# Head roots as a TensorE product, a reordered batch step and epilogues moved into the feed-forward tiles

## The chip, the cores and the metric

The kernel runs on one NeuronCore of a Trainium2 chip. The metric is the device time of one execution in microseconds (us), the median of three runs. Engines: PE (TensorE), DVE (VectorE), ACT (ScalarE), POOL (GpSimd) and SP (the queue that issues most DMAs).

## What is computed

The input is 8 sequences of 256 rows of 512. First comes an mLSTM cross attention with 16 heads of 32, whose query is the normalised `x` and whose keys and values are both `ctx`; then a feed-forward network (FFN) whose activations and weights are quantised in blocks of 32.

```python
Cn = C / (normalizer + EPS)
h = jnp.einsum('bhst,bhtd->bhsd', Cn, vh)
mu = h.mean(-1, keepdims=True)
var = ((h - mu) ** 2).mean(-1, keepdims=True)
hn = (h - mu) * jax.lax.rsqrt(var + EPS)
hn = hn * ln_scale.reshape(1, nh, 1, dh)
...
x = x + _L0_xattn_ref(_layernorm(x, axis=-1), ctx_2048, ctx_2048, ...)
x = x + _L0_ffn_ref(_layernorm(x, axis=-1), ...)
```

## The kernel before, in words

The work is tiled by 128 rows, so a sequence b has two chunks. Every engine has its instructions written out by hand in program order, and each runs them first in, first out; semaphores tie them together. There is no scheduler. An instruction that waits holds back all that stands behind it on its engine.

There are four stretches.

1. **Loading** (`pre_step`, eight times): x is normalised (`x_stats` on DVE, `x_rsqrt` on POOL, `x_norm` on ACT), x and ctx are transposed on PE, the gate products (`gates`) are accumulated, and one unit of the FFN's down weights is quantised per step. A weight unit passes through `w_front`, `w_pow`, `w_round` (DVE), `round_const` (ACT), `w_back` (POOL), `w_transpose` (PE) and an evacuation (ACT).
2. **Gates**: short operations on ACT and DVE turn the gates into decay tables; these go to DRAM and come back as `movt` and `statt` (`load_decay`).
3. **Batch steps** (`step`, b = 0 to 7). On PE: `heads` for chunk 0 (four, n = 0 to 3), `decay` 4 and 5, `centre`, `qk`, `x_transpose`, `state`, `decay` 6 and 7, `heads` for chunk 1 (n = 4 to 7), `inter`, a weight transpose, and then `decay` and `qk` of the next sequence. ACT takes exponentials of the decays (`exps`) and copies PSUM out (`copy_h`, `copy_v`, `copy_state`). DVE multiplies scores and decays (`c_mult`, four and four). Beside this the epilogue of the sequence before runs: `square` (ACT), `head_var` (DVE), `head_power` (ACT), `head_rsqrt` (POOL), `head_norm` (DVE, L1040), the product with the layer scale (POOL, L616), the residual (POOL, L621), `x1_stats` (DVE), `x1_rsqrt` (POOL), `x1_norm` (ACT, L826), `x1_round` (DVE), `back_x` (POOL). Two weight units are quantised in each step.
4. **FFN**: 16 tiles, each in two halves h. Per half PE does `p_transpose` of the tile before, `gate`, `up` and `down` of the tile before; ACT does `silu` and copies; DVE does `pair` (L1104, the block maxima, L1113, L1116); POOL does `back_p` (L679). The epilogue of sequence 7 and the rounding of sequence 6 run around the first tiles.

`settle` adds one to a semaphore nobody waits on. `ch.link` makes an engine wait for its own last instruction.

## Time and profile before

| | us |
|---|---|
| median of three runs | 553.61 |
| lowest, highest | 552.74, 558.61 |
| the profiled execution | 553.07 |
| its span, first to last instruction | 551.3 |

```profile
PE 454.0 (82%) x3465; PEld 300.7 (55%) x3465; DVE 432.6 (78%) x615; ACT 244.9 (44%) x343; POOL 245.2 (44%) x231
PE   0597795599789696969788785399999999999984
DVE  3769888478797897978787965997788788788880
POOL 2444531323635536273736563543454443443433
PEclk9767886589859586776859697899999999999996
```

The first line gives each engine's busy time and share of the span. The others cut the span into 40 slices; a digit is the busy share in tenths (PEclk: the granted TensorE clock, in tenths of 2.4 GHz). The batch steps are slices 8 to 24, where the clock digit swings once per step; the FFN is slices 25 to 40.

### The profile page before, as it was taken

What the parts mean: (1) busy time and instruction counts of PE and PEld (TensorE: products, weight loads), DVE (VectorE), ACT (ScalarE), POOL (GpSimd) and SP (SyncE); (2) the same over time, 40 slices, a digit from 0 to 9 for tenths busy, and PEclk for the clock granted to TensorE, in tenths of its full rate; (3) what the DMA queues carried; (4) which work ended last, traced back from release to release, by engine and by line L of the source; (5) the groups of instructions that cost most, each with busy time, mean ns of one, the idle gap of its engine ahead of it and who ended that gap; (6) DMA issues with size and microseconds to landing.
All of it is one profiled execution on the core that took longest, in us unless ns stands there. A gap on an engine that the chain in (4) does not pass through costs nothing.

```text
span 551.3 us, 10415 instructions
## 1 busy us (share of the span) xinstructions
PE 454.0 (82%) x3465; PEld 300.7 (55%) x3465; DVE 432.6 (78%) x615; ACT 244.9 (44%) x343; POOL 245.2 (44%) x231
## 2 busy tenths in 40 slices
PE   0597795599789696969788785399999999999984
PEld 0497795287657484757566562144444444444441
DVE  3769888478797897978787965997788788788880
ACT  2466664247264353545364544234434344344341
POOL 2444531323635536273736563543454443443433
PEclk9767886589859586776859697899999999999996
DMA  6655621412321414050421101201111111112111
GB/s 164 214 173 175 224 97 38 137 54 85 134 62 60 137 42 144 11 173 22 134 62 55 42 26 52 77 0 40 38 38 53 61 38 38 38 38 75 39 38 39
DMA packets 30564, 43.70 MB, mean 79 GB/s; under 512 B 6980, under 2 KB 11972, under 8 KB 30532
## 3 DMA queue, kind: packets, MB, share of 16 engines
q1 hardware_dynamic: 30532, 43.26, 24.3%
q8 instruction: 21, 0.34, 0.3%
q14 instruction: 11, 0.09, 0.1%
HBM read 34.41 MB, written 8.85 MB: 78 GB/s over the span
## 4 chain that ended last, share of the span: by engine, by line
PE 42%; issue 20%; POOL 17%; DVE 13%; ACT 4%; DMA 3%; POOLq 1%; SPq 1%; DVEq 0%; ACTq 0%
PE psA L1335 9%; PE psC L1362 9%; PE psA L1344 9%; PE psB L1354 3%; POOL wq L559 3%; POOL early L616 3%; PE psA L1234 2%; PE psC L1214 2%; DMA early<-in_x_dram 2%; POOL xc L649 2%; DVE wy L952 2%; DVE wq L955 1%; POOL qs L644 1%; PE psC L1173 1%; POOL rs L553 1%
## 5 line engine op out<-in xcount | busy, mean ns | idle before, releaser
L679 POOL TENSOR_TENSOR kTa<-kTa,ps 128x1024 bf16<-128x1024 bf16 x32 | 61.2, 1912 | 102.7 <-DVE kTa L1116 102.7
L1262 PE MATMUL psA<-vp,DC 128*128 128x128 f32 x512 | 73.7, 312 | 2.1 <-DVE DC L1019 2.1
L559 POOL TENSOR_TENSOR wq<-wq,ws 128x1024 bf16<-128x1024 bf16 x24 | 50.6, 2108 | 54.9 <-DVE wq L955 54.9
L1262 PEld LDWEIGHTS psA<-vp,DC 128*128 128x128 f32 x512 | 71.4, 227 | 4.0 <-issue 4.0
L1335 PE MATMUL psA<-WgT,qTa 128*128 128x512 bf16 x256 | 63.7, 394 | 7.5 <-ACT hf L813 3.9
L1362 PE MATMUL psC<-WdT,kTa 128*128 128x512 bf16 x256 | 62.2, 387 | 2.4 <-ACT kTa L879 2.4
L1344 PE MATMUL psA<-WuT,qTa 128*128 128x512 bf16 x256 | 61.3, 383 | 0.0
L879 ACT ACTIVATE kTa<-psB 128x1024 bf16<-128x1024 bf16 x32 | 32.8, 1024 | 54.5 <-PE psB L1354 54.2
L1019 DVE SCALAR_TENSOR_TENSOR DC<-psA,DC 128x512 f32<-128x512 f32 x64 | 41.7, 686 | 15.7 <-PE psA L1234 8.3
L1104 DVE TENSOR_TENSOR kTa<-kTa,psA 128x1024 f32<-128x1024 f32 x32 | 39.0, 1220 | 18.2 <-PE psA L1344 18.2
L804 ACT ACTIVATE DC<-psB 128x512 f32<-128x512 f32 x64 | 37.6, 597 | 23.6 <-PE psB L1248 23.2
L1113 DVE TENSOR_TENSOR qTa<-kTa,pinv 128x1024 fp8e4<-128x1024 f32 x32 | 41.1, 1285 | 4.9 <-DVE pinv L933 4.3
L1362 PEld LDWEIGHTS psC<-WdT,kTa 128*128 128x128 bf16 x256 | 25.3, 99 | 33.4 <-issue 3.1
L873 ACT ACTIVATE kTa<-psA 128x1024 f32<-128x1024 f32 x32 | 32.8, 1024 | 23.7 <-PE psA L1335 23.7
L1344 PEld LDWEIGHTS psA<-WuT,qTa 128*128 (+1 forms) x256 | 25.3, 99 | 31.3 <-issue 2.0
L1335 PEld LDWEIGHTS psA<-WgT,qTa 128*128 (+1 forms) x256 | 24.4, 101 | 32.3 <-ACT hf L813 4.0
L1182 PE MATMUL psC<-identb,wq 128*128 128x128 bf16 x192 | 21.3, 279 | 24.3 <-POOL wq L559 24.3
L927 DVE TENSOR_REDUCE pam<-kTa 128x32 f32<-128x1024 f32 x32 | 39.0, 1220 | 1.1
L1234 PE MATMUL psA<-qTa,kTa 32*128 32x128 f32 x512 | 25.4, 349 | 12.8 <-ACT hf L813 12.8
L1246 PE MATMUL psB<-mask,identb 128*128 128x512 bf16 x64 | 30.5, 477 | 5.7 <-DMA statt<-gate_split_scratch 5.7
L726 ACT ACTIVATE wm<-wm,wbase 128x1024 f32<-128x1024 f32 x24 | 27.5, 1147 | 16.1 <-DVE wm L947 16.1
L826 ACT ACTIVATE early<-early,nb,rs 128x512 f32<-128x512 f32 x16 | 12.1, 806 | 50.6 <-POOL nb L554 50.6
(131 smaller groups left out, 849.7 us busy)
## 6 DMA issues: line engine op xcount, KB each, us to landing
early<-in_x_dram SPq DMA_DIRECT2D x16, 512.0 KB, 4.1
early<-in_ctx_dram SPq DMA_DIRECT2D x8, 512.0 KB, 4.6
wraw<-in_L_ffn_w_down_dram SPq DMA_DIRECT2D x8, 512.0 KB, 5.5
wraw<-in_L_ffn_w_gate_dram SPq DMA_DIRECT2D x8, 512.0 KB, 4.2
...
```

Source lines behind the costliest of these rows:

```text
L559: nc.gpsimd.tensor_tensor(blocks(wq[p][:, :]), blocks(wq[p][:, :]), spread(ws4[p][:, :], UB), ALU.mult).then_inc(wq_ready.sem, 1)
L679: nc.gpsimd.tensor_tensor(blocks(pd[h]), blocks(pc[h]), spread(ps4[h][:, :], PB), ALU.mult).then_inc(pq_ready.sem, 1)
L804: nc.scalar.activation(DC[n % DCN][:, :], psB[n % 2][:, :], ACT.Exp).then_inc(d_exp.sem, 1)
L927: return nc.vector.tensor_reduce(am, src, AX.X, ALU.max, apply_absolute_value=True)
L1019: nc.vector.scalar_tensor_tensor(out=DC[n % DCN][:, :], in0=psA[:, n % HPC, :], scalar=float(DH) ** -0.5, in1=DC[n % DCN][:, :], op0=ALU.m ...
L1104: nc.vector.tensor_tensor(pr, sg, psA[:, PC:2 * PC, :].rearrange("p a b -> p (a b)"), ALU.mult).then_inc(p_ready.sem, 1)
L1113: fch.link(nc.vector.tensor_tensor(blocks(p8), blocks(pr), spread(pinv[:, :], PB), ALU.mult, saturate=False))
L1234: last = nc.tensor.matmul(psA[:, j, i4 * P:(i4 + 1) * P], kTa[r, b, i4, c * P:(c + 1) * P], qTa[r, b, i4, c * P:(c + 1) * P], start=True, ...
L1262: last = nc.tensor.matmul(psA[:, j, to:to + P], DC[n % DCN][:, i4 * P:(i4 + 1) * P], values[:, left:left + P], start=i4 == 0, stop=c == 0, ...
L1335: last = nc.tensor.matmul(psA[:, a, :], xqT[q][:, b, c * P:(c + 1) * P], WgT[:, c, h * PW + a * E:h * PW + (a + 1) * E], start=c == 0, sto ...
L1344: last = nc.tensor.matmul(psA[:, PC + a, :], xqT[q][:, b, c * P:(c + 1) * P], WuT[:, c, h * PW + a * E:h * PW + (a + 1) * E], start=c == 0 ...
L1362: last = nc.tensor.matmul(psC[p][:, :], pTs[h][:, k * P:(k + 1) * P], WdT[:, PK * h + k, :], start=h == 0 and k == 0, stop=h == 1 and k == ...
```

## The change

- **Roots times layer scale.** Before, DVE multiplied the heads by the roots (SBUF by SBUF, one operation of 128x1024) and POOL multiplied the result by the broadcast layer scale. Now PE transposes the roots of a sequence (`root_transpose`), ACT copies them out (`copy_root`), and PE multiplies them with a block-diagonal table `ltab` of the layer scale (`scale_root`, one fp32 product of 32x128 by 32x512 per chunk), which gives roots times scale as a matrix in PSUM. DVE multiplies each chunk of heads with it (`head_norm`, two of 128x512, PSUM by SBUF). POOL's product is gone.
- **The batch step** is put in another order on all engines. On PE the gate-weight transpose stands behind `decay` 5, the other weight transpose behind the next sequence's `qk` and `decay`s. On ACT `x1_norm` stands behind the next sequence's exponentials. On DVE `w_pow` stands between the two `head_norm`s and `w_front` ahead of `x1_stats`. On POOL `w_back` stands ahead of the residual.
- **Start.** The x, weight and ctx loads are issued in another order on SP and the small constants from ACT's queue; the layer-scale load is 32 rows instead of 128; POOL makes its tables after the second `x_rsqrt`; a decay waits only for its own chunk's loads; `qk(0, 0)` goes ahead of the first decay.
- **FFN.** `x1_round` of sequence 6 and the whole epilogue of sequence 7 are cut up and put between the `pair`s of tiles 0 to 6; `x_transpose` moves to tiles 5 and 9. The roots of sequence 7 come from a POOL power of 128x16 per chunk (`last_power`) instead of ACT's logarithm and exponential and POOL's refinement.

```diff
+            def last_power(b, c):
+                gp.wait_ge(hv_ready.sem, hv_ready.at(b, 1))
+                last = nc.gpsimd.tensor_tensor(sm[:, 0, c, :], sm[:, 3, c, :], mhalf[:, 0:1].broadcast_to([P, NH]), ALU.pow)
+                if c == NCH - 1:
+                    last.then_inc(hr_ready.sem, 1)
...
-                ch.link(nc.gpsimd.tensor_tensor(hn, hn, lns[:, :].unsqueeze(1).broadcast_to([P, NCH, E]), ALU.mult))
...
+            def copy_root(b):
+                act.wait_ge(r_mm.sem, r_mm.at(b, 0))
+                act.wait_ge(rt_mm.sem, rt_mm.at(b, 1))
+                nc.scalar.activation(rT[:, :], psC[1][0:DROW, 0:NCH * P], ACT.Copy).then_inc(rt_ev.sem, 1)
...
+            def head_norm(b, p, c, bank):
+
+                ve.wait_ge(r_mm.sem, r_mm.at(b, c + 1))
+                nc.vector.tensor_tensor(sq[:, c], hf[p][:, c, :, 0:DH],
+                                        psC[bank][:, :].rearrange("p (h d) -> p h d", d=DH),
                                         ALU.mult).then_inc(hn_ready.sem, 1)
...
+            def root_transpose(b):
+
+                root = sm[:, :, :, :].rearrange("p k c h -> p (k c h)")
+                pe.wait_ge(hr_ready.sem, hr_ready.at(b, 1))
+                for c in range(NCH):
+                    last = nc.tensor.transpose(psC[1][0:DROW, c * P:(c + 1) * P], root[:, c * NH:c * NH + DROW], ident[:, :])
+                last.then_inc(rt_mm.sem, 1)
+
+            def scale_root(b, c, bank):
+                pe.wait_ge(rt_ev.sem, rt_ev.at(b, 1))
+                nc.tensor.matmul(psC[bank][:, :], rT[:, c * P:(c + 1) * P], ltab[:, :], start=True, stop=True).then_inc(r_mm.sem, 1)
...
 def decay(b, p, n):
                 c, j = divmod(n, HPC)
-                if n == 0:
-                    pe.wait_ge(d_ld, 16 * NCH * (1 + SPLIT) * b + 16 * NCH * (1 + SPLIT))
+                if j == 0:
+                    pe.wait_ge(d_ld[p][c], 16 * (1 + SPLIT) * (b // 2 + 1))
```

POOL's batch step, and its FFN part up to the loop:

```diff
             def step(b, p, n, first, last):
                 if not first:
                     head_rsqrt(b - 1)
+                w_back(2 * b + B + 1, 1)
                 if not first:
                     residual(b - 1)
                 if not last:
                     carry_q(b + 1, 1 - p)
-                w_back(2 * b + B + 1, 1)
                 if not first:
                     x1_rsqrt(b - 1)
                 if not last:
+                    weigh(b + 1, 1 - p)
                     w_back(2 * b + B + 2, 0)
-                    weigh(b + 1, 1 - p)
...
+            back_p(0, 0)
+            last_power(B - 1, 0)
+            back_p(0, 1)
+            last_power(B - 1, 1)
+            back_p(1, 0)
+            back_p(1, 1)
             residual(B - 1)
```

DVE in the first FFN tiles:

```diff
             pair(0, 0)
+            head_var(B - 1, 1)
+            pair(0, 1)
+            pair(1, 0)
+            head_norm(B - 1, 1, 0, 1)
+            pair(1, 1)
+            head_norm(B - 1, 1, 1, 1)
+            pair(2, 0)
+            x1_amax(B - 2, fch)
+            pair(2, 1)
+            x1_scale(B - 2, fch)
+            pair(3, 0)
+            x1_clamp(B - 2)
+            pair(3, 1)
             x1_stats(B - 1)
```

**PE, the middle of a batch step.** `cen` is `centre`, `qTa,kTa` is `qk`, `xc` is `x_transpose`, `ctc` is `state`, `mask` and `movt` are the two products of a `decay`, `DC4` is the first of `heads` for chunk 1. Before:

```order
L1214 MATMUL psC0<-cen,kTa 128x128 x4
L1234 MATMUL psA<-qTa,kTa 128x128 x16
L1280 MATMUL psC1<-identb,xc 128x128 x8
L1224 MATMUL psC0<-vw,ctc 32x33 x16
L1246 MATMUL psB0<-mask,identb 128x512
L1248 MATMUL psB0<-movt,statt 128x512
L1246 MATMUL psB1<-mask,identb 128x512
L1248 MATMUL psB1<-movt,statt 128x512
L1262 MATMUL psA<-vp1,DC4 128x128 x4
```

The same place now, with `sm` for `root_transpose` and `ltab` for `scale_root`:

```order
L1292 MATMUL psC0<-cen,kTa 128x128 x4
L1312 MATMUL psA<-qTa,kTa 128x128 x16
L1366 MATMUL psC1<-ident,sm 32x128 x2
L1302 MATMUL psC0<-vw,ctc 32x33 x16
L1371 MATMUL psC1<-ltab,rT 128x512
L1324 MATMUL psB0<-mask,identb 128x512
L1326 MATMUL psB0<-movt,statt 128x512
L1324 MATMUL psB1<-mask,identb 128x512
L1326 MATMUL psB1<-movt,statt 128x512
L1371 MATMUL psC0<-ltab,rT 128x512
L1358 MATMUL psC1<-identb,xc 128x128 x8
L1340 MATMUL psA<-vp1,DC4 128x128 x4
```

Both root products now stand in front of the chunk 1 heads, the second behind two decays.

**DVE, the middle of a batch step.** `wq` ends `w_round`; `DC` is the first `c_mult` of chunk 1. Before:

```order
L952 SCALAR_TENSOR_TENSOR wy<-wy,wm 128x1024
L96 REGISTER_ALU
L954 REGISTER_ALU
L955 SCALAR_TENSOR_TENSOR wq<-wy,wm 128x1024
L1040 TENSOR_TENSOR early<-hf,sm 128x1024
L1017 REGISTER_ALU
L1019 SCALAR_TENSOR_TENSOR DC<-psA,DC 128x512
```

Now:

```order
L997 SCALAR_TENSOR_TENSOR wy<-wy,wm 128x1024
L96 REGISTER_ALU
L999 REGISTER_ALU
L1000 SCALAR_TENSOR_TENSOR wq<-wy,wm 128x1024
L1087 REGISTER_ALU
L1088 TENSOR_TENSOR early<-hf,psC 128x512
L990 REGISTER_ALU
L992 TENSOR_SCALAR wm<-wy 128x1024
L1088 TENSOR_TENSOR early<-hf,psC 128x512
L1064 REGISTER_ALU
L1066 SCALAR_TENSOR_TENSOR DC<-psA,DC 128x512
```

The chunk 1 `c_mult`s stand behind both `head_norm`s, and so behind both root products.

**ACT, the end of a batch step.** `early<-early,nb,rs` is `x1_norm`, `hf` is `copy_h` of chunk 1, `DC` an `exps` of the next sequence. Before:

```order
L726 ACTIVATE wm<-wm,wbase 128x1024
L826 ACTIVATE early<-early,nb,rs 128x512 x2
L813 ACTIVATE hf<-psA 128x4x4x33
L730 REGISTER_ALU
L731 REGISTER_ALU
L731 ACTIVATE WuT<-psC 128x4x256
L803 ISA
L804 ACTIVATE DC<-psB 128x512
```

Now:

```order
L832 REGISTER_ALU
L833 ACTIVATE DC<-psB 128x512
L832 REGISTER_ALU
L833 ACTIVATE DC<-psB 128x512
L860 ACTIVATE early<-early,nb,rs 128x512 x2
L759 REGISTER_ALU
L760 REGISTER_ALU
L760 ACTIVATE WuT<-psC 128x4x256
L854 ACTIVATE early<-hf 128x1024
```

`x1_norm` has moved from ahead of `copy_h` to behind the fourth exponential of the next sequence.

## Rows read from the trace of the kernel before

**Rows 1.** Windows: length, busy of PE, PEld, DVE, ACT, POOL, granted clock, DMA share, GB/s

```profile
129.75:159.55 29.80, 23.74 (x247) 18.29 (x245) 25.23 (x39) 14.21 (x24) 15.21 (x15) 0.83 0.31 99
159.55:313.27 153.72, 129.75 (x1241) 97.17 (x1240) 129.31 (x192) 74.01 (x116) 78.39 (x75) 0.72 0.25 80
313.27:335.36 22.09, 16.32 (x205) 12.88 (x205) 14.77 (x25) 12.31 (x21) 13.14 (x13) 0.96 0.15 48
335.36:442.10 106.74, 93.21 (x500) 43.73 (x501) 88.30 (x111) 40.43 (x45) 46.85 (x33) 0.94 0.12 40
```

**Rows 2.** Chain of waits inside one batch step: start us, us, what

```profile
234.11 2.37 POOL early L616
...
245.27 0.80 ACT early L826
246.07 0.51 ACT hf L813
```

**Rows 3.** Timeline, DVE, same step: start us, us, engine line, tiles [idle before]

```profile
232.81 1.22 DVE L1040 TENSOR_TENSOR early<-hf,sm 128x1024 f32<-128x1024 f32 x1
...
239.54 1.29 DVE L1048 BATCH_NORM_STATS2 st<-early 128x6 f32<-128x512 f32 x2 [2.25 <-POOL early L621]
...
246.78 1.21 DVE L927 TENSOR_REDUCE xam<-early 128x32 f32<-128x1024 f32 x1
...
251.97 1.28 DVE L1019 SCALAR_TENSOR_TENSOR DC<-psA,DC 128x512 f32<-128x512 f32 x2
```

**Rows 4.** Windows, PE alone, same step: length, busy, granted clock, DMA share, GB/s

```profile
223.90:227.90 4.00, 4.00 (x22) 0.52 0.00 0
227.90:239.90 12.00, 12.00 (x167) 1.00 0.19 67
239.90:242.70 2.80, 0.04 (x4) 0.77 0.63 209
```

**Rows 5.** Timeline, PE: one step's products, and both `heads` groups

```profile
111.00 5.77 PE L1262 MATMUL psA<-vp,DC 128*128 128x128 f32 x32
...
229.40 0.38 PE L1246 MATMUL psB<-mask,identb 128*128 128x512 bf16 x1
...
230.67 1.16 PE L1214 MATMUL psC<-cen,kTa 128*128 128x128 f32 x8
...
231.75 1.17 PE L1234 MATMUL psA<-qTa,kTa 32*128 32x128 f32 x32
...
235.08 3.84 PE L1262 MATMUL psA<-vp,DC 128*128 128x128 f32 x32
...
238.85 1.09 PE L1272 MATMUL psA<-Sst,qs 32*128 32x33 f32 x32
```

**Rows 6.** Groups by line: busy us, mean ns of one, idle before

```profile
L1163 PE MATMUL psC<-brow,qs 1*128 1x512 f32 x2 | 2.0, 1122 | 3.3 <-POOL vw L587 3.3
L553 POOL TENSOR_TENSOR rs<-rt,mhalf 128x2 f32<-128x2 f32 x16 | 12.1, 758 | 1.3
L804 ACT ACTIVATE DC<-psB 128x512 f32<-128x512 f32 x64 | 37.6, 597 | 23.6 <-PE psB L1248 23.2
```

**Rows 7.** Timeline of POOL and DVE at one moment

```profile
216.30 1.91 POOL L559 TENSOR_TENSOR wq<-wq,ws 128x1024 bf16<-128x1024 bf16 x1 [2.52 <-DVE wq L955]
...
217.29 0.96 DVE L930 TENSOR_SCALAR xs<-xam 128x32 int32<-128x32 int32 x1
```

**Rows 8.** Timeline, PE, the first decay of sequence 0

```profile
104.20 0.58 PE L1246 MATMUL psB<-mask,identb 128*128 128x512 bf16 x1 [5.74 <-DMA statt<-gate_split_scratch]
```

**Rows 9.** Timeline of one half tile of the steady FFN: PE, DVE and POOL

```profile
521.71 1.22 DVE L1104 TENSOR_TENSOR kTa<-kTa,psA 128x1024 f32<-128x1024 f32 x1 [0.53 <-PE psA L1344]
...
526.24 0.69 DVE L1116 TENSOR_SCALAR kTa<-qTa 128x1024 bf16<-128x1024 fp8e4 x1 [0.16 <-DVE qTa L1113]
527.19 1.91 POOL L679 TENSOR_TENSOR kTa<-kTa,ps 128x1024 bf16<-128x1024 bf16 x1 [3.90 <-DVE kTa L1116]
...
529.16 0.62 PE L1354 MATMUL psB<-identb,kTa 128*128 128x128 bf16 x8
```

259 lines of the change are left out of this document (162 added, 97 removed).

## The prediction

> **What bounds the kernel now.** I read the windows first, for how long each stretch is. From the first `c_mult` of sequence 1 to that of sequence 2 are 29.8 us, the five steps after it take 153.72, or 30.74 each, the last one takes 22.09 up to the first gate product, and eight FFN tiles take 106.74 [rows 1]. No engine fills a batch step: DVE is busy for 129.31 of 153.72 us. So a step is a loop of waits, and the chain of waits says which: POOL's product with the layer scale (2.37), the residual behind it, the POOL square root, ACT's `x1_norm`, and only then `copy_h`, which stood behind `x1_norm` on ACT [rows 2]. On DVE's timeline the same loop shows as a wait of 2.25 us for the residual [rows 3]. I call the start of a step's first `c_mult` time 0 (251.97 in rows 3, and 221.24 one step of 30.73 earlier). `head_norm` then starts at 11.6, `x1_round` at 25.5.
>
> The clock matters as much. It fell to 1.2 GHz after 2.8 us without a product, and was back at 2.4 GHz about 3.8 us after the `heads` of the next step had begun [rows 4]. Sixteen fp32 products of `heads` last 5.77 us at the low level and 3.84 at the high one [rows 5].
>
> In the FFN a half tile takes 5.8 us. From the start of `pair` on DVE to `p_transpose` on PE are 7.45 us, and POOL's `back_p` ends just when PE asks for it; DVE's own part lasts 5.2, which leaves it 0.6 per half [rows 9].
>
> **Loading and gates.** The constants now arrive early, but POOL's tables stand behind a second `x_rsqrt`, and the gate weights behind the tables; the second transposes on PE come out at the same time. Zero, with 1.5 either way. At the end of loading, `gates(7)` no longer has a weight transpose ahead of it, but two stand behind it with an ACT copy between them, and ACT's gate operations stand behind both copies: +0.7.
>
> **The first step.** PE waited 5.74 us for the decay tables [rows 8]. The first decay now needs four loads of the eight: four issues at 0.3, -1.2. `qk(0, 0)` (1.7) goes ahead of that wait and the weight transpose (1.0 at the low clock) behind the heads. So the chunk 0 heads begin 3.8 us earlier than at 111.0 [rows 5]. Behind them DVE is the limit, and its order `w_pow`, `c_mult`, `w_front`, `w_round` brings sequence 1's first `c_mult` 3.65 us earlier. POOL's tables for `ltab` have long ended by then. -3.65.
>
> **The batch steps.** DVE loses the idle 2.25 and POOL the 2.37. But DVE's second four `c_mult`s now stand behind both `head_norm`s, these behind two root products on PE, and these behind the chunk 0 heads of the same step. With time 0 as above:
>
> - `c_mult` 0.68, then `heads`. PE has been idle for about 7 us by then (below), so the clock is low. At 5.77 to 3.84 the first 3.8 us do 2.5 us worth of work, the rest runs at the high clock: 5.1. That is 5.8.
> - Two decays 1.27 (229.40 to 230.67), weight transpose 0.5 (as `p_transpose` in rows 9), `centre` 1.08, `qk` 1.11 [rows 5]: 9.8.
> - Root transpose 0.3 and `copy_root` 0.4, estimates below the 0.6 of an `exps` [rows 6]: 10.5.
> - First root product. The nearest row is the bias product, also fp32 with 512 columns, 2.0 us for its two passes at the low clock [rows 6], so 1.0 at the high one and 2.0 as the other end: 11.5. Two decays, 12.8; second root product, 13.8; second `head_norm` 0.7 with its start: 14.6. `w_pow` between the two waits for POOL's `w_back` until 12.4, which this covers.
> - `c_mult` 0.68, `heads` 3.77, `inter` 1.09, `copy_h` 0.7, `qk` 1.15, decay 0.64, `centre` 1.08, two decays 1.27, the last `exps` 0.65, `x1_norm` 1.6 (two of 0.80), and `x1_round` with `w_pow` 4.4 (5.19 between 246.78 and 251.97, less the 0.8 it stood still there): 17.0.
>
> The loop closes at 31.6. DVE's own work would close it at 27 to 28; it now waits some 3 us ahead of `x1_round` for `x1_norm`. The weight transpose ends at 25.5 and PE waits until 32.3, which is why the clock is low. +0.9 for each of five steps, +4.5. The ends: with the clock high throughout the heads last 3.77 and the loop takes 30.3; if it returns only after the heads and two decays, 32.9. Sequence 1's step starts on a busy PE, so 30.3 against 29.8: +0.5. In the last step the second half is `c_mult`, `heads`, `inter`, `copy_h`, `x1_norm`, and the evacuation of the last weights (1.0), 23.5 against 22.09: +1.4.
>
> **The FFN.** At its front the roots, the POOL product and the waits of DVE behind them no longer come before the pairs; the first `pair` starts 6.2 us after the first gate product, not 9.4. Put between the pairs are `head_var` 2.3, two `head_norm` 1.4, two `x1_amax` 4.4, two `x1_scale` 2.5, `x1_stats` 1.6 and two `x1_clamp` 1.3, 13.5 in all. Each delays the next `p_transpose` by its length less the 0.6 of slack, and the scale and clamp also take the port ahead of `back_p`. PE gets two root products and their transposes, 2.3. Walking the halves through with 5.2 for a pair, 1.91 for `back_p` and 1.73 for a group of eight products, tile 3 starts 8 us earlier than before and tile 8 0.5 later than before.
>
> That was with `last_power` at 0.7, the time of the power on two columns [rows 6]. It has sixteen. POOL's multiply on two columns takes 0.2, so the power itself costs 0.25 a column, and by columns it would be 4.2 each. Both stand ahead of a `back_p`, and the root transpose waits for the second.
>
> Does DVE stand still meanwhile? While POOL's `w_back` ran, a DVE operation of 0.18 took 0.96 us and ended with it [rows 7]. So it does. The Trainium skill (page "SBUF — State Buffer", on the shared port pair) says that whichever of the two starts first holds the pair for its whole instruction and the other fully blocks; by that rule the FFN would be 5.9 us longer at 4.2 each, and about 4 without it. The trace agrees with it.
>
> So +0.5 to +5.9, and as no row decides on the width I take the middle, +3.2.
>
> **The sum**: 0.7 - 3.65 + 0.5 + 4.5 + 1.4 + 3.2 = +6.65. The profiled execution took 553.07 us (span 551.3), 0.5 below the median of 553.61, so 560.3 on the scale of the median. I forecast 560.
>
> **Rivals.** (1) Not slower. The point that decides is whether the chunk 0 heads run at the high clock, or the chain over DVE, `x1_rsqrt` and `x1_norm` ends last. Then a step takes 30.3 to 30.7, five of them -2 to 0, and with a short `last_power` the sum is 0.7 - 3.65 + 0.5 - 1 + 0.5 + 1 = -2: 551.5 us. For it speaks that in the step of sequence 1 the clock stood at 0.83 on average [rows 1]; against it, that the heads must wait for a `c_mult` which stands behind all of `x1_round`. Price up to 553. (2) The change does what it removes: PE's part costs less than I put it, DVE becomes the limit of the step, at 28.4 us with small waits. Five steps and the one before give -13, and the rest as above 0 to +1: about 540. Against it stands DVE's fixed order, with two waits per step that DVE itself can't fill. (3) The root products run at the low clock too, 2.0 each, with `centre` and `qk` doubled: a step of 35 us, +21, and 577 in all.
>
> **Chances.** The forecast with its neighbours (555 to 569) 0.52, rival 1 0.30, rival 2 0.11, rival 3 0.07. By 1%, 5.5 us, which is about what can be told from no change: faster 0.14 (rival 2 and the lower edge of 1), within 0.35, slower 0.51. The range reaches from 545 to 571: below it is most of rival 2, above it rival 3. The forecast's own range is 555 to 569.
>
> **What would show it.** In the profile of the changed kernel: first `c_mult` to first `c_mult` 31 to 32.5 us, DVE waiting 2 to 4 us for ACT ahead of `x1_round` and a fraction ahead of the second `head_norm`, no wait ahead of `x1_stats`; the granted clock at 0.50 in the first 4 to 5 us of each step and high after; the first decay 1 us or so earlier and the first step 3 to 4. `last_power` between 0.7 and 4.2. In the FFN, PE waits of 1 to 3 us ahead of `p_transpose` in tiles 1 to 6. I would be wrong if the step closes without PE, if the clock stays high across the wait for `c_mult`, or if the inserted DVE work finds room in the first tiles that I did not see.

## The result, and the profile after

The changed kernel takes 581.49 us (median of four runs, 579.08 to 589.25) against 553.17 for the kernel before in the same comparison: 1.055 times as long, 95% interval 1.051 to 1.060. (The ratio goes by the fast runs alone, without the one of 589.25, and so is not the quotient of the two medians.) I had forecast 560 us with a range up to 571: slower is right, the size is not. The profiled execution took 579.77 us, its span is 578.2.

The windows of the same stretches as in [rows 1], now of the changed kernel (length, busy of PE, PEld, DVE, ACT and POOL, granted clock, DMA share, GB/s):

```profile
126.44:160.78 34.34, 25.80 (x267) 18.55 (x266) 27.38 (x40) 18.40 (x29) 15.74 (x16) 0.89 0.27 88
160.78:331.34 170.56, 130.51 (x1270) 99.14 (x1270) 123.94 (x197) 77.40 (x120) 73.25 (x71) 0.80 0.23 71
331.34:357.17 25.83, 21.41 (x206) 17.24 (x207) 12.16 (x23) 10.70 (x18) 9.65 (x11) 0.82 0.19 62
357.17:470.63 113.46, 98.22 (x502) 45.49 (x503) 90.45 (x114) 39.48 (x43) 52.27 (x30) 0.92 0.10 33
```

Sequence 1's first `c_mult` comes 3.3 us earlier (126.44 for 129.75). Its step takes 34.34 for 29.80, the five steps behind it 170.56 for 153.72 (34.1 each for 30.7), the last one 25.83 for 22.09, eight FFN tiles 113.46 for 107.0 (counted to the gate product, at 442.36 in the kernel before). That is -3.3 + 4.5 + 16.8 + 3.7 + 6.5 and -1.4 behind it, 26.8 us: the difference of the spans is 26.9. The -1.4 comes with TensorE's clock in the last eight products of the kernel: they took 1.90 us here, at a granted clock of 1.00, and 3.60 in the kernel before, at 0.50.

One step of it on DVE, from the `c_mult` at 228.95 (the time 0 of [rows 3]) to the next at 263.07 (start us, us, line, tiles, [idle before]):

```profile
228.95 2.48 DVE L1066 SCALAR_TENSOR_TENSOR DC<-psA,DC 128x512 f32<-128x512 f32 x4
...
241.82 0.69 DVE L1088 TENSOR_TENSOR early<-hf,psC 128x512 f32<-128x512 f32 x1 [2.63 <-PE psC L1371]
...
243.83 0.69 DVE L1088 TENSOR_TENSOR early<-hf,psC 128x512 f32<-128x512 f32 x1 [0.72 <-PE psC L1371]
244.44 2.48 DVE L1066 SCALAR_TENSOR_TENSOR DC<-psA,DC 128x512 f32<-128x512 f32 x4
...
258.65 1.22 DVE L972 TENSOR_REDUCE xam<-early 128x32 f32<-128x1024 f32 x1 [4.70 <-ACT early L860]
...
263.07 1.28 DVE L1066 SCALAR_TENSOR_TENSOR DC<-psA,DC 128x512 f32<-128x512 f32 x2
```

DVE waits 2.63 and 0.72 us for the two root products and 4.70 for `x1_norm`. The same step on PE:

```profile
229.78 6.26 PE L1340 MATMUL psA<-vp,DC 128*128 128x128 f32 x32 [6.77 <-DVE DC L1066]
...
239.74 0.39 PE L1366 MATMUL psC<-ident,sm 128*32 128x128 f32 x2
...
240.66 1.12 PE L1371 MATMUL psC<-ltab,rT 32*128 32x512 f32 x2
...
242.68 1.12 PE L1371 MATMUL psC<-ltab,rT 32*128 32x512 f32 x2
...
245.27 5.39 PE L1340 MATMUL psA<-vp,DC 128*128 128x128 f32 x32 [0.92 <-DVE DC L1066]
```

The two root products of a step, one for each chunk, cost what I put them at. Both `heads` groups, though, are longer than 3.84 us. The windows of PE alone say why (length, busy, granted clock, DMA share, GB/s):

```profile
229.78:234.50 4.72, 4.72 (x22) 0.50 0.00 0
234.50:236.04 1.54, 1.54 (x13) 0.86 0.00 0
236.04:244.35 8.31, 8.18 (x102) 1.00 0.30 83
244.35:245.27 0.92, 0.00 (x0) 0.94 0.33 125
245.27:248.50 3.23, 3.23 (x15) 0.50 0.04 13
248.50:256.90 8.40, 8.21 (x106) 1.00 0.63 201
```

The first group ran at 1.2 GHz for 4.72 of its 6.26 us. In the second half, where I had 3.77 us at the high level, the clock stood at 1.2 GHz again for 3.23 us, after a wait of only 0.92. And on ACT, the place of `x1_norm` (L860) behind four exponentials of the next step (L833):

```profile
252.36 0.60 ACT L833 ACTIVATE DC<-psB 128x512 f32<-128x512 f32 x1
254.36 0.60 ACT L833 ACTIVATE DC<-psB 128x512 f32<-128x512 f32 x1 [1.41 <-PE psB L1326]
...
256.02 1.20 ACT L833 ACTIVATE DC<-psB 128x512 f32<-128x512 f32 x2
257.12 1.51 ACT L860 ACTIVATE early<-early,nb,rs 128x512 f32<-128x512 f32 x2
```

### The profile page after: what moved, and what is told of

Its sections match the earlier page's. It is cut to its first block, busy times and chain, and to the rows that moved or that the text cites. A ratio compares the mean times of both kernels' runs of the same rounds, so it can differ in the third digit from the quotient of the medians.

```text
span 578.2 us, 10388 instructions
## 1 busy us (share of the span) xinstructions
PE 467.1 (81%) x3513; PEld 310.1 (54%) x3513; DVE 427.9 (74%) x623; ACT 248.9 (43%) x349; POOL 241.5 (42%) x223
## 4 chain that ended last, share of the span: by engine, by line
PE 53%; DVE 23%; issue 9%; POOL 5%; DMA 4%; ACT 4%; DVEq 1%; SPq 1%; POOLq 0%; ACTq 0%
PE psA L1340 15%; PE psA L1438 7%; PE psA L1447 6%; PE psC L1465 4%; DVE wam L972 4%; DMA early<-in_x_dram 3%; DVE qTa L1169 3%; PE psA L1312 3%; DVE kTa L1160 3%; PE psB L1326 3%; PE psB L1324 2%; PE psC L1292 2%; POOL kTa L689 2%; PE psC L1371 2%; PE psB L1457 2%
## 5 line engine op out<-in xcount | busy, mean ns | idle before, releaser
L1340 PE MATMUL psA<-vp,DC 128*128 128x128 f32 x512 | 88.6, 353 | 48.5 <-DVE DC L1066 48.5
L1340 PEld LDWEIGHTS psA<-vp,DC 128*128 128x128 f32 x512 | 86.0, 266 | 51.7 <-issue 48.5
L689 POOL TENSOR_TENSOR kTa<-kTa,ws 128x1024 bf16<-128x1024 bf16 x32 | 63.2, 1976 | 119.9 <-DVE kTa L1172 119.9
L833 ACT ACTIVATE DC<-psB 128x512 f32<-128x512 f32 x64 | 38.0, 596 | 26.4 <-PE psB L1326 25.7
L1169 DVE TENSOR_TENSOR qTa<-kTa,winv 128x1024 fp8e4<-128x1024 f32 x32 | 39.2, 1225 | 4.8 <-DVE winv L978 2.5
L1447 PEld LDWEIGHTS psA<-WuT,qTa 128*128 128x128 bf16 (+1 forms) x256 | 25.4, 99 | 32.2 <-issue 3.4
L1465 PEld LDWEIGHTS psC<-WdT,kTa 128*128 128x128 bf16 x256 | 24.8, 98 | 32.0 <-issue 1.4
L1438 PEld LDWEIGHTS psA<-WgT,qTa 128*128 128x128 bf16 (+1 forms) x256 | 25.2, 104 | 29.8 <-issue 9.2
L972 DVE TENSOR_REDUCE wam<-kTa 128x32 f32<-128x1024 f32 x32 | 39.0, 1220 | 1.1
L1457 PE MATMUL psB<-identb,kTa 128*128 128x128 bf16 x256 | 20.1, 223 | 16.2 <-POOL kTa L689 15.5
L1088 DVE TENSOR_TENSOR early<-hf,psC 128x512 f32<-128x512 f32 x16 | 11.0, 686 | 28.8 <-PE psC L1371 28.8
L1457 PEld LDWEIGHTS psB<-identb,kTa 128*128 128x128 bf16 x256 | 15.6, 99 | 29.4 <-issue 23.9
```

The lines of the kernel that those rows point to most:

```text
L689: nc.gpsimd.tensor_tensor(blocks(pd[h]), blocks(pc[h]), spread(ps4[h][:, :], PB), ALU.mult).then_inc(pq_ready.sem, 1)
L833: nc.scalar.activation(DC[n % DCN][:, :], psB[n % 2][:, :], ACT.Exp).then_inc(d_exp.sem, 1)
L972: return nc.vector.tensor_reduce(am, src, AX.X, ALU.max, apply_absolute_value=True)
L1169: fch.link(nc.vector.tensor_tensor(blocks(p8), blocks(pr), spread(pinv[:, :], PB), ALU.mult, saturate=False))
L1340: last = nc.tensor.matmul(psA[:, j, to:to + P], DC[n % DCN][:, i4 * P:(i4 + 1) * P], values[:, left:left + P], start=i4 == 0, stop=c == 0, ...
L1438: last = nc.tensor.matmul(psA[:, a, :], xqT[q][:, b, c * P:(c + 1) * P], WgT[:, c, h * PW + a * E:h * PW + (a + 1) * E], start=c == 0, sto ...
```

## The experiments

Each was compared with the kernel before on its own chip, so the ratios are what compares. "Step" is the mean of the five steps that begin with sequence 2, from DVE's timeline of one profiled execution; "FFN" is from the first gate product to the end of the span. Where two intervals overlap (e1 and e2, e3 and e4, o4 to o6), the times do not tell the kernels apart, and only the steps do.

| kernel | median us | ratio to before (95%) | step | FFN |
|---|---|---|---|---|
| before | 553.17 | 1 | 30.74 | 215.9 |
| changed | 581.49 | 1.055 (1.051 to 1.060) | 34.11 | 221.0 |
| e1: 24 idle products | 574.17 | 1.041 (1.034 to 1.047) | 32.52 | 221.1 |
| e2: 24 and 4 | 569.23 | 1.036 (1.028 to 1.044) | 30.84 | 226.0 |
| e3: no matrix | 569.67 | 1.035 (1.030 to 1.040) | 32.67 | 219.4 |
| e4: no matrix, 24 and 4 | 570.78 | 1.035 (1.029 to 1.041) | 32.67 | 218.7 |
| o2: statistics first | 582.02 | 1.056 (1.045 to 1.066) | 34.20 | 221.1 |
| o3: o2 with e2 | 569.80 | 1.032 (1.021 to 1.043) | 30.85 | 226.0 |
| o4: o2, `x1_norm` early | 566.08 | 1.030 (1.021 to 1.039) | 31.41 | 223.5 |
| o5: o4, 12 and 4 | 565.98 | 1.024 (1.016 to 1.032) | 30.87 | 223.5 |
| o6: o4, no matrix | 562.80 | 1.019 (1.013 to 1.026) | 31.69 | 219.3 |
| b1: before, `x1_norm` late | 571.55 | 1.036 (1.028 to 1.045) | 34.03 | 219.5 |
| s1: before, new start | 549.46 | 0.998 (0.995 to 1.001) | 30.44 | 215.6 |
| s2: s1, 9 and 6 | 549.67 | 0.998 (0.993 to 1.002) | 29.84 | 215.7 |
| m1: s1, rounding late | 555.91 | 1.013 (1.006 to 1.019) | 31.96 | 218.2 |
| m2: m1, three moves kept | 554.35 | 1.009 (1.006 to 1.012) | 30.85 | 222.5 |
| m3: changed, rounding late | 565.48 | 1.027 (1.021 to 1.032) | 31.87 | 222.8 |
| m4: m3, in the other gap | 563.65 | 1.022 (1.017 to 1.028) | 30.78 | 223.6 |
| f1: no power in the FFN | 575.71 | 1.044 (1.035 to 1.053) | 34.19 | 219.0 |

### The clock: e1 and e2

```diff
+            def warm(n):
+                for _ in range(n):
+                    nc.tensor.matmul(psB[0][:, :].rearrange("p (i t) -> p i t", i=HC), identb[:, :],
+                                     mask[:, :].unsqueeze(1).broadcast_to([P, HC, P]), start=True, stop=True,
+                                     skip_group_check=True)
...
                 w_transpose(2 * b + B + 1, 1, rows_order)
+                if not last:
+                    pe.wait_ge(d_exp.sem, d_exp.at(b + 1, 3))
+                    warm(24)
```

> The changed kernel with 24 products more in every step but the last: 128x512 bf16 into a PSUM bank that nothing reads, put behind the last weight transposes, so that TensorE is busy in the 6.77 us that it now waits for the coefficients of the first half. Nothing that is used is computed otherwise. Theory A (the loop of heads and coefficients sets the step, and the heads of chunk 0 cost 6.26 us there in place of 3.84 because TensorE idled just ahead of them): the granted clock is 1.00 in these heads, they take 3.9 us, the step falls from 34.1 by 2.4 to 31.7 us, the kernel from 579.8 by some 7 x 2.4 = 17 to 563 us (565 at worst, if the products run past the wait by .5 us in each step). Rival B (the new waits for the roots set the step, and the heads have slack): heads faster, step still 34, time 579 to 582. Rival C (the products themselves delay the heads): slower than 582 us.

```diff
                     x_transpose(b - 2)
+                pe.wait_ge(d_exp.sem, d_exp.at(b, 7))
+                warm(4)
                 for k in range(HPC, 2 * HPC):
```

> The same with 4 such products more ahead of the heads of chunk 1, where the clock fell to .50 for 3.3 us. Theory A: these heads go from 5.38 to 3.9 us, the step to 31.7 - 1.5 = 30.2 us, less what the 4 products take beyond the wait of .92 us (4 x .32 = 1.3 us, so .4 us); the kernel to 553 to 557 us. If the fall of the clock there does not come from the wait right ahead of it, the heads of chunk 1 stay at 5.4 us and the kernel is .4 us a step slower than the kernel with 24 products, 566 us. Rival B: 579 to 582 us.

In e1 the chunk 0 heads took 3.81 us, as expected, but the step fell by 1.6 us, not 2.4. Some 0.5 of the missing 0.8 is in those of chunk 1, which took 5.2 or 6.3 us in turn, 5.9 on average, for 5.4. Rival B is out all the same. In e2 both are at the high level in three of the five steps (30.45 us each); in the other two (31.4 each) the clock averaged 0.95. Its windows of PE, first and second part of one of the three:

```profile
228.69:242.09 13.40, 12.85 (x139) 1.00 0.20 60
242.09:259.14 17.05, 15.28 (x145) 1.00 0.35 112
```

The mean step is 30.84, 3.3 us less. So the low clock in the heads is on the loop, with 3.3 of its 3.9 us (2.4 and 1.5). The kernel gained 12 us only (10.2 between the two spans), not the 20 of the last six steps. Two places took the rest. Sequence 1's step, in which PE has no long wait to fill, took 38.67 us for 34.34, because the idle products stood ahead of the heads:

```profile
130.62 5.34 PE L1380 MATMUL psB<-mask,identb 128*128 128x512 bf16 x24
135.80 3.73 PE L1340 MATMUL psA<-vp,DC 128*128 128x128 f32 x32
```

And the FFN took 226.0 us for 221.0: 3.7 up to tile 8, with a granted clock of 0.89 in its first 107 us, and 1.3 in the last eight products (3.21 us for 1.90). Why the clock and the first tiles lose there stays open.

### The matrix: e3 and e4

e3 leaves the order as it is; the head norm reads the roots from SBUF, POOL multiplies by the layer scale:

```diff
-                ve.wait_ge(r_mm.sem, r_mm.at(b, c + 1))
-                nc.vector.tensor_tensor(sq[:, c], hf[p][:, c, :, 0:DH],
-                                        psC[bank][:, :].rearrange("p (h d) -> p h d", d=DH),
+                ve.wait_ge(hr_ready.sem, hr_ready.at(b, 1))
+                nc.vector.tensor_tensor(sq[:, c], hf[p][:, c, :, 0:DH], spread(sm[:, 0, c, :], NH),
                                         ALU.mult).then_inc(hn_ready.sem, 1)
...
+                ch.link(nc.gpsimd.tensor_tensor(hn, hn, ltab[:, :].unsqueeze(1).broadcast_to([P, NCH, E]), ALU.mult))
```

> The changed kernel, order and placement as they are, without the root matrix: no root transposes, no copy of them, no root products, no wait of TensorE for the head norm; the head norm reads the root of each head broadcast from SBUF, and GpSimd multiplies by the layer scale ahead of the residual sum, as the kernel before does. Theory A with the matrix as the cause: root transposes, two products and the waits of VectorE for them (2.63 + .72 us) leave the loop, the step falls from 34.1 by 2.2 to 3.3 us, to 31 to 32 us, the kernel to 557 to 566 us. Theory A with the new order as the cause: the step keeps 33.5 to 34.1 us (the products filled idle time of TensorE, and the heads of chunk 1 now run at the low clock too), the kernel stays at 576 to 580 us. GpSimd has 1.9 us more to do in each step and is nowhere waited for longer than now in either.

> Both together: no root matrix, and the 24 and 4 idle products. If the two costs are separate, the savings add: the step at 30.2 less what the third kernel saves, 28 to 30 us, the kernel at 540 to 555 us, under the kernel before where it is 552. If the idle time of TensorE is one cost that either of them takes away, it comes out like the better of the two alone, within 3 us.

Without the matrix the step is 32.67, and idle products change nothing (32.67). e4 did not do what it was meant to in chunk 0: its 24 products ended up to 3.5 us ahead of those heads, which took 5.3 to 6.7 us in four steps of five. But e3 alone shows that the heads' clock does not set this step: its chunk 1 heads took 3.81 us in some steps and 5.4 in others, and every one of the five steps took 32.65 to 32.69. The loop is another one there: DVE is busy 28.7 us of it and waits 2.71 for `x1_norm`. It is busier because three short instructions stand still while POOL works on the product with the layer scale, the residual and the weight block. The timeline of DVE in e3:

```profile
235.78 2.40 DVE L982 TENSOR_SCALAR wm<-wy 128x1024 int32<-128x1024 int32 x1
...
242.34 1.62 DVE L965 TENSOR_SCALAR ws<-wam 128x32 int32<-128x32 int32 x1
244.00 1.19 DVE L968 TENSOR_SCALAR winv<-ws 128x32 int32<-128x32 int32 x1
```

They take 0.69, 0.18 and 0.18 elsewhere. DVE's row adds up: without the matrix 3.35 us of waits for the root products go and 2.0 of the wait for `x1_norm`, and DVE is busy 3.9 us longer (28.7 for 24.8), 1.45 in all, the difference of the steps. So the matrix both costs and gives; once the loop is opened otherwise, the step with it is even the shorter one, 31.41 (o4) against 31.69 (o6). As a whole kernel the one without it is not slower even then (1.019 against 1.030, intervals overlapping), since its FFN is the shorter, 219.3 against 223.5.

### The place of `x1_norm`: o2, o3, o4, b1

o2 only puts `x1_stats` ahead of `w_front` on DVE again; o3 is that with e2's idle products.

```diff
-                if not last:
-                    w_front(2 * b + B + 3, 1, b + B // 2 + 1)
                 if not first:
                     x1_stats(b - 1)
                 if not last:
+                    w_front(2 * b + B + 3, 1, b + B // 2 + 1)
                     w_round(2 * b + B + 2, 0)
```

> The changed kernel with one thing put back: VectorE takes the statistics of x1 ahead of the first half of the next weight block, as the kernel before does, not behind it. The step of VectorE is 24.8 us busy and else waits; the wait for the normalized x1 is 4.71 us of it (2.71 us in the kernel without the root matrix, 3.12 with the idle products). Theory D (VectorE's own row closes the loop: after the statistics it has 2.4 us of work and then waits until GpSimd and ScalarE have handed back the normalized x1, 5.5 us later): with 3.7 us more work between, the wait goes, and what is left of it is what ScalarE's place for the normalization (behind four exponentials of the next step, at the low clock) keeps. The step falls from 34.1 by 2.0 to 4.0 us, the kernel by 12 to 28 us, to 552 to 568 us. Theory A (the heads of the two halves at the low clock set the step, whatever VectorE waits for): the wait ahead of the rounding only becomes one ahead of the coefficients, the step stays at 33.5 to 34.1, the kernel at 576 to 581 us.

> The same with the 24 and 4 idle products of the second kernel tried. Theory D: the step was 30.46 us there with 3.12 us of wait for the normalized x1; without that wait 27.3 to 28 us, the kernel at 568 - 6 x 2.8 = 548 to 554 us; the idle products now outlast the wait that they fill, so up to 1 us a step of this is lost. Theory A: step 30 to 30.5 us, kernel 565 to 569 us.

Both of my expectations (theory D) fell: the statistics came 2.6 us earlier, but the wait only went from 4.7 to between 4.2 and 4.5 us, and the step stayed; o3 came out like e2. `x1_norm` was not late for its statistics, but for the four exponentials ahead of it on ACT. o4 moves it:

```diff
                 if not last:
                     exps(b + 1, 0)
+                if not first:
+                    x1_norm(b - 1)
+                if not last:
                     exps(b + 1, 1)
...
                     exps(b + 1, 3)
-                if not first:
-                    x1_norm(b - 1)
```

> The changed kernel with two places put differently: the statistics of x1 ahead of the first half of the weight block on VectorE (which by itself moved nothing: 34.15 us a step, and the wait for the normalized x1 only fell from 4.71 to 4.43), and ScalarE's normalization of x1 right behind the first exponential of the next step, where ScalarE waits 1.41 us for TensorE, not behind the fourth. Theory L (the loop that sets 34.1 us is: heads of chunk 1, the next step's first products and decays, exponentials 0 to 3, the normalization behind them, VectorE's rounding of x1, and behind it the coefficients that the heads of chunk 0 wait for; every link waits for the one ahead of it): the normalized x1 is there about 2.6 us sooner, VectorE's wait falls from 4.4 to 1.5 to 2.5 us, the step to 31 to 32.3 us, the kernel from 581 to 560 to 570 us. Theory A (only TensorE's products and their clock): step 34, kernel 578 to 583 us.

The step is 31.41 and the kernel 2.5% of before's time faster than the changed one. ACT's timeline in o4, where the norm fills what was a wait of 1.41:

```profile
244.29 0.60 ACT L833 ACTIVATE DC<-psB 128x512 f32<-128x512 f32 x1
244.79 1.51 ACT L860 ACTIVATE early<-early,nb,rs 128x512 f32<-128x512 f32 x2
```

A part of the gain is the clock's. In three of the five steps the chunk 1 heads ran at the high level (3.81 us) and the step took 30.8 to 30.9; in the other two they took 6.5 and 5.3 us and it took 32.4 and 32.0. So the new place gives 1.7 to 2.1 us with these heads at the low clock, and 3.2 with them at the high one.

The mirror image is b1, the kernel before with that one move and nothing else of the change:

```diff
-                if not first:
-                    x1_norm(b - 1)
                 copy_h(b, p, 1)
...
                     exps(b + 1, 3)
+                if not first:
+                    x1_norm(b - 1)
                 square(b, p)
```

> The kernel before with one line moved as the change moves it: ScalarE normalizes x1 behind the four exponentials of the next step, not ahead of the copy of the heads. Theory L (exponentials, normalization, rounding, coefficients and heads in one loop): exponential 3 ends at 223.8 in the step that begins with the coefficients at 221.2, so the normalization ends at 225.3 in place of 215.3, the rounding (3.9 us and the next block's power of two, .7) behind it at 230, where the coefficients stand at 221.2 now; less the 1.5 us that the copy of the heads comes sooner. The step gets 4 to 7 us longer, 35 to 38 us, the kernel 576 to 596 us. Rival M (the place costs only together with the root matrix and the changed order on TensorE): step 30.5 to 31.5, kernel 549 to 556 us.

The step is 34.03 us, 3.3 longer than in the kernel before, as the one move does by itself. That it equals the changed kernel's 34.11 is chance: b1's chunk 1 heads run at the high clock (3.81 us), it has no wait for root products, and it keeps the wait of 2.25 us for the residual. I had expected a step 4 to 7 us longer. Its rows: ACT behind the exponentials, and DVE waiting for it ahead of `x1_round`, where the kernel before does not wait:

```profile
224.32 0.60 ACT L804 ACTIVATE DC<-psB 128x512 f32<-128x512 f32 x1 [0.48 <-PE psB L1248]
224.81 1.51 ACT L826 ACTIVATE early<-early,nb,rs 128x512 f32<-128x512 f32 x2
```

```profile
226.35 1.22 DVE L927 TENSOR_REDUCE xam<-early 128x32 f32<-128x1024 f32 x1 [5.83 <-ACT early L826]
```

### Both at once: o5 and o6

> The same with idle products (12 ahead of the heads of chunk 0, 4 ahead of those of chunk 1), so that both heads run at the high clock. Theory L: the 2.4 and 1.5 us of the heads come off a loop that has lost 2.6 us already, until VectorE's 25.9 us of work and its waits for the roots set it: step 28 to 29.5 us, kernel 550 to 558 us. If the loop is no longer the heads' but VectorE's, the products bring under 1 us a step.

> The new places without the root matrix (the roots broadcast from SBUF, the layer scale on GpSimd). In the kernel without the matrix VectorE is busy 28.7 us of its 32.67 us step, 3.9 us of it three instructions that stand still beside GpSimd's products (1.62, 1.19 and 2.40 us in place of .33, .18 and .69), and waits 2.71 us for the normalized x1, which comes as soon as its root is there. With the statistics 3.7 us sooner this wait goes: step 30 us (29.5 to 30.5), kernel 566 - 6 x 2.6 = 550 to 555 us, if VectorE's row sets it. If instead the heads set it (7 us of wait ahead of those of chunk 0 now), the step stays over 32 us.

Neither came as far as I expected. In o5 DVE has no wait for `x1_norm` left, but in the step that I read, the inverse of the scales stood still 1.83 us (for 0.18) beside POOL, the root products still made it wait 1.80 and 0.72, and the heads of chunk 0 took 5.4 us again, at a granted clock of 0.69: the 12 products ended 3.3 us ahead of them. The chunk 1 heads took 3.81 us in every step, and every step 30.8 to 30.9, what o4 has where they do. In o6 the wait for the residual came back (2.79 us).

### The start: s1, s2

s1 is the kernel before with the changed kernel's order of loads, tables and first products; s2 adds idle products, 9 ahead of the second weight block's transposes and 6 ahead of the next `qk`.

```diff
-            decay_qk(0, 0)
+            qk(0, 0)
...
+            decay(0, 0, 0)
+            decay(0, 0, 1)
...
-                if n == 0:
-                    pe.wait_ge(d_ld, 16 * NCH * (1 + SPLIT) * b + 16 * NCH * (1 + SPLIT))
+                if j == 0:
+                    pe.wait_ge(d_ld[p][c], 16 * (1 + SPLIT) * (b // 2 + 1))
```

> The kernel before with the start of the changed kernel alone. By the trace of the changed kernel its first coefficients of sequence 1 come 3.3 us sooner (predicted 2.95): kernel 3 us under before, 548 to 550 us, steps and feed-forward part as before (30.7 and 107 us for tiles 0 to 7). The rival: the 3.3 us are lost again at the first loads of the weights, no difference. Beside the kernel with this start and the idle products (549.7 us, step 29.8) it tells what those products bring: if this one has 30.7 us a step and comes out at 549 too, the products' gain is lost elsewhere.

> The kernel before with the changed kernel's start (order of the loads, constants on ScalarE's queue, a semaphore for each part of the decay loads, first products of queries and keys ahead of the tables) and with idle products in each step: 9 where TensorE waits 2.8 us ahead of the transposes of the second weight block, and 6 where it waits 2.0 us ahead of the next step's products of queries and keys. The start is worth 3.3 us by the trace of the changed kernel. If the low clock from these waits to the end of chunk 0's heads costs the step (products of queries and keys 2.09 in place of 1.17, centring 2.08 for 1.16, six decays .6 for .39, heads 5.6 for 3.84: 5 us of TensorE time), the step goes from 30.7 to 27 to 29 us and the kernel to 535 to 543 us. If VectorE's row sets it (25.9 us busy, waits of 2.25 for x1 and 1.2 for exponentials), only the 1.2 us go: step 29.5 us, kernel 541 to 546 us. If the products do nothing, 548 to 550 us.

The start is worth 0.2% with an interval from -0.5% to +0.1%, 1.0 us and at most 2.8. One trace can't show it: in 17 profiled executions with the new start the first `c_mult` of all lies between 103.4 and 112.2 us, in the two with the old one (before, b1) at 107.1 and 105.9. From there to sequence 1's first are 20.5 to 22.0 us with the new start (23.7 in s2), 22.7 and 21.7 with the old. In s2 the 0.6 us a step that the products bring do not show in the time: the two steps ahead of the five are 2.5 and 2.0 us longer with them (23.7 for 21.2 and 31.7 for 29.8), much as sequence 1's is in e2.

### The rounding elsewhere: m1 to m4

m1 takes `x1_round` out of its place ahead of the next coefficients in the kernel before; m2 keeps three moves of the change on top; m3 and m4 do it in the changed kernel.

```diff
                     head_var(b - 1, 1 - p)
+                if not (isinstance(b, int) and b < 2):
+                    x1_round(b - 2)
...
-                if not (first or last):
-                    x1_round(b - 1)
```

> The kernel before with the changed start, and with VectorE's rounding of x1 taken out of the place ahead of the coefficients: it stands in the next step behind the head variance, GpSimd's last product on it and TensorE's transposes of it follow it there (they belonged to the next step's second half anyway), the normalization stands at the end of ScalarE's step, and the statistics behind the first half of the weight block. No arithmetic is changed. Theory L: the next coefficients no longer wait for the residual sum, the statistics, GpSimd's root, the normalization and the rounding; the 2.25 us for the residual sum are covered by the weight block. The step falls from 30.4 to 27 to 29 us, where VectorE's 25.9 us of work or the waits of TensorE for the second weight block (2.80 us) set it, and the kernel to 549 - 6 x 1.5 to 3.4, 529 to 541 us. Rival: the heads at the low clock (5.6 us) and TensorE's wait for the second weight block set the step, 30 us, kernel 547 to 550 us.

> The same, and three moves of the change kept: TensorE takes the next step's decays, products of queries and keys and centring ahead of the transposes of the second weight block, GpSimd scales that block back ahead of the residual sum, and ScalarE copies it out behind the exponentials. If TensorE's wait for that block stands in the new loop, 1 to 2.5 us a step less than the kernel without these three moves (step 26.5 to 27.5, kernel 525 to 533 us); if VectorE's row is the bound by then, the same within 1 us a step.

> The changed kernel with VectorE's rounding of x1 and GpSimd's product behind it moved from the end of the step into the next step, behind the head variance; nothing else is changed, the root matrix stays. Theory L, and the matrix pays by what it takes off GpSimd: the wait of 4.71 us for the normalized x1 goes, the coefficients of the next step wait for nothing but their own exponentials, and VectorE's row sets the step with 25.9 us of work, 1 to 2 us of it standing beside GpSimd, and up to 1 us of waits for the root products: 27.5 to 29 us, kernel 579.5 - 6 x 5.1 to 6.6 = 540 to 549 us, under both kernels at the lower end. If the step stays at 30.8 us as in the kernel before with the same move, the matrix brings nothing: kernel 558 to 561 us.

> The changed kernel with the rounding of x1 one step later, as in the kernel before this one (31.87 us a step, 565 us), but behind the coefficients of the second half on VectorE, with GpSimd's product behind the carried queries and TensorE's transposes of it behind the next step's decays. If the loop is the one of both halves' coefficients: first half 13 us of VectorE's work in place of 17.6, second half 15 to 16: step 28.5 to 30 us, kernel 562 - 6 x 1.9 to 3.4, 541 to 552 us. If the step stays between 31.5 and 32.5 us, something else sets it (GpSimd's row, or the power and lock beside it), kernel 561 to 567 us.

m3 and m4 took 2.2 and 3.3 us off the changed kernel's step, and none of the four beats the kernel before. The steps at the ends changed too: sequence 1's has no rounding in it any more (25.7 us in both, for 34.3), the last has one more (28.1 and 28.9, for 25.8).

In m1 another wait took the place of the one that was opened. DVE is busy for 25.4 of 31.6 us and waits 4.3 for POOL's `w_back`, which stands behind the layer scale's product, the residual and the carried queries:

```profile
242.12 0.18 DVE L932 TENSOR_SCALAR ws<-wam 128x32 int32<-128x32 int32 x1 [4.29 <-POOL wq L552]
```

m2 puts `w_back` ahead of the residual. That wait is gone, and now DVE's own row is the bound, busy for 28.9 of 30.9 us; it has become longer by what stands still beside POOL. m2's DVE timeline, behind the second half's coefficients:

```profile
235.67 2.32 DVE L949 TENSOR_SCALAR wm<-wy 128x1024 int32<-128x1024 int32 x1
237.92 1.21 DVE L929 TENSOR_REDUCE wam<-wraw 128x32 f32<-128x1024 f32 x1
239.16 1.10 DVE L932 TENSOR_SCALAR ws<-wam 128x32 int32<-128x32 int32 x1
240.29 1.19 DVE L935 TENSOR_SCALAR winv<-ws 128x32 int32<-128x32 int32 x1
```

These four took 2.3, 1.2, 1.1 and 1.2 us, 3.6 us more in all than where they are undisturbed (0.69, 1.21, 0.18, 0.18). In the kernel before DVE is busy for 25.9 us of a step; in m2, m3 and m4 it is 28.9, 28.4 and 27.4, with waits of 0.8 to 2.8 us left. I expected a step of 26.5 to 30 in all four and got 30.8 to 32.0: in these three, part of each wait that was opened came back as DVE standing still, in m1 as a wait for POOL. In none of the four were the chunk 1 heads at the high clock throughout (5.1 to 6.7 us in nearly every step); no run separates what that costs from DVE's row.

### The power in the FFN: f1

```diff
-                last = nc.gpsimd.tensor_tensor(sm[:, 0, c, :], sm[:, 3, c, :], mhalf[:, 0:1].broadcast_to([P, NH]), ALU.pow)
+                last = nc.gpsimd.tensor_tensor(sm[:, 0, c, :], sm[:, 3, c, :], mhalf[:, 0:1].broadcast_to([P, NH]), ALU.mult)
```

> The changed kernel with the power of the last step's 128x16 roots on GpSimd (2.89 and 3.00 us) made a product; it leaves out the last inverse root and computes nothing else otherwise. Prediction's step on the feed-forward part: if the power and the lock that it holds on VectorE (waits of .99 to 1.95 us in three instructions there) make the 6.5 us that tiles 0 to 8 got longer, they come back: tiles 0 to 8 at 108 to 110 us in place of 113.5, kernel 575 to 577 us. If the place of the residual, of the copies and of TensorE's root products among the tiles makes them (waits of 2.52, 2.26 and 2.38 us ahead of the transposes), 1 to 2 us come back, kernel 578 to 580 us.

The windows from the first gate product to the third `p_transpose`, and from there to tile 6, of the changed kernel:

```profile
357.17:390.01 32.84, 25.68 (x100) 10.74 (x101) 19.85 (x27) 8.64 (x9) 11.59 (x5) 0.79 0.01 1
390.01:451.86 61.85, 54.73 (x299) 26.12 (x298) 53.67 (x69) 23.68 (x26) 30.51 (x20) 0.97 0.13 43
```

and of f1:

```profile
356.33:385.17 28.84, 23.93 (x101) 10.27 (x102) 19.87 (x27) 8.53 (x9) 6.12 (x5) 0.82 0.01 1
385.17:447.03 61.86, 54.73 (x299) 25.98 (x298) 53.68 (x69) 23.69 (x26) 30.53 (x20) 0.97 0.13 43
```

The powers cost 4.0 us, all of it in the first stretch; the second is the same to 0.01, so the eight tiles take 109.5 us, as the first of the two expectations had it. 2.5 of the 6.5 us of the eight tiles are left for the epilogues' places, not shown one by one. The whole FFN is only 2.0 us shorter (219.0 for 221.0), since the last eight products ran at the low clock in f1 (3.59 us) and at the high one in the changed kernel (1.90).

## Why the prediction was right and wrong, step by step

**The loop was the right one.** I had the step close over the coefficients, the heads of chunk 0, the root products, the second head norm, the coefficients and heads of chunk 1, the exponentials, `x1_norm` and `x1_round`. That is what e2, o4 and b1 show: shorten a link (e2 -3.3, o4 -2.7) and the step is shorter; put `x1_norm` behind the exponentials (b1, +3.3) and the loop is there without the matrix. The fraction of a wait ahead of the second head norm, none ahead of `x1_stats`, and `last_power` at 2.9 are as listed; the wait ahead of `x1_round` is the expected one but longer, 4.70 us for 2 to 4.

**The step that failed is the sizes of two terms in it**, both the clock. From 228.95 to the second head norm's end I had 14.6 us, it took 15.5; the chunk 0 heads are 1.0 too long (6.10 us to the next product for 5.1), and the rest comes to -0.1. The 1.0 has two causes. The clock came back after 4.7 us, not 3.8. And I had read 5.77 us [rows 5] as the time of sixteen products at the low level, but that group is mixed, as its two windows show:

```profile
111.00:115.14 4.14, 4.14 (x21) 0.50 0.14 45
115.14:116.77 1.63, 1.63 (x16) 1.00 0.00 0
```

The profile has two records for each of these products. In the 4.14 us at 1.2 GHz a record starts every 0.21 us, at 2.4 GHz every 0.11. The step of [rows 4], with 3.88 us at the low level, took 5.5 us to the next product, so 0.4 of the 1.0 was to be had from the trace before and 0.6 is the later return of the clock. The second half I had at 17.0, it took 18.6; the chunk 1 heads have 1.55 of that (5.32 for 3.77): I had put them at the high level without a reason, and gave no price for the low one. The other terms hold to 0.2 or 0.3: root transpose and `copy_root` took 0.9 for 0.7, the two decays and the second root product 2.0 for 2.3. Together 2.5 us a step: 34.1, not 31.6. Over five steps 12.3 us are missing, and in the last step (25.8 for 23.5) 2.3. e2, where both groups run at the high clock, comes to 30.84, near the 30.3 that I gave as the end with a high clock. My upper end was 32.9, since I let the low clock vary in chunk 0 alone; a range for the clock has to hold for every group of products on the loop.

**Sequence 1's step** I took for a high clock throughout, 30.3; it took 34.34. Its chunk 0 heads were at the high level (3.79 us), those of chunk 1 were not (5.29), its first half began with a wait for exponentials, `w_pow` stood in it beside POOL (2.12 us for 0.69), and its second half is the loop's 18.5. 4.0 us of the miss.

**The start**: -2.95 expected, -3.3 in the trace, -1.0 (at most -2.8) by s1. That it came out in the trace proves little.

**The FFN**: +3.2 expected between +0.5 and +5.9; measured +6.5 up to tile 8, past the upper end, and +5.1 for the whole, with the -1.4 of the last products' clock. The epilogues' part, which I had at +0.5 with a short power, is +2.5 by f1. The power on sixteen columns took 2.89 and 3.00 us, between the 0.7 and 4.2 that I had from two columns, and cost 4.0 in all. What I derived from the port lock was wrong in the case of the power. The rows of the changed kernel:

```profile
367.92 1.91 POOL L689 TENSOR_TENSOR kTa<-kTa,ws 128x1024 bf16<-128x1024 bf16 x1 [14.99 <-DVE kTa L1172]
367.95 1.95 DVE L1076 TENSOR_TENSOR sm<-sm,gT 128x32 f32<-128x32 f32 x1
...
378.80 3.00 POOL L620 TENSOR_TENSOR sm<-sm,mhalf 128x16 f32<-128x16 f32 x1
...
379.15 0.18 DVE L975 TENSOR_SCALAR ws<-wam 128x32 int32<-128x32 int32 x1
...
379.69 1.23 DVE L1169 TENSOR_TENSOR qTa<-kTa,winv 128x1024 fp8e4<-128x1024 f32 x1
...
381.86 0.61 PE L1366 MATMUL psC<-ident,sm 128*32 128x128 f32 x2 [2.26 <-POOL sm L620]
```

Beside `back_p` a DVE operation of 0.2 us took 1.95 and ended with it; beside the power DVE's instructions kept their 0.18 and 1.23. The power costs through PE, which waited 2.26 us for its result, and at the low clock behind that. The Trainium skill's rule of the shared port pair (page "SBUF — State Buffer", "SBUF: two separate sides") is that the later of the two fully blocks, where DVE's operation is in a 2-port mode or has two SBUF inputs, and in the latter case where GpSimd's reads SBUF. It is borne out by the first pair of rows, and the rows of e3 fit it; beside the power it is not, as the product of 1.23 us reads two SBUF tiles and was not held.

**The rivals.** Rival 3 came nearest with its 577 us (step 35, 34.1 measured), by the wrong mechanism: it doubled the root products, `centre` and `qk`, which all ran at the high level; it was the heads of chunk 1. Rival 1's point of decision, whether the chunk 0 heads run at the high clock, was decided against it by the row of 6.26 us. Even so the kernel would have been slower: with these heads at 3.81 us e1 is at 1.041, as chunk 1's were at the low clock too, and e2, with both at the high one in most steps, is at 1.036. Rival 2 needed DVE's row to close the step. m4 comes near that, with 30.8 us, not 28.4: DVE is busy for 27.4 of it and still waits 1.6 for the root products. The range missed because I gave 0.07 to all that was slower than 569. The two upper ends that I had stated, 32.9 for the step and +5.9 for the FFN, add up to 569.5 us only; what was missing was a price at the low clock for chunk 1's heads, in sequence 1's step too.

Open: why the FFN, whose code is the same in b1, m1 and m2 as before, took 219.5, 218.2 and 222.5 us there for 215.6 to 215.9 in before, s1 and s2. All of it lies ahead of tile 2, which starts 41.2, 40.0 and 44.6 us behind the first gate product, for 37.4. In b1 the last step is 3.6 us shorter instead (18.5 for 22.1), so there the time seems only to have moved across the border; in m1 and m2 it has not. The 5 us that the changed kernel's FFN is longer may hold some of that.
